# Four weight matrices loaded in 128-byte instead of 512-byte runs, with plain instead of spread columns, and GpSimd's combining of them moved ahead of four bias adds

## The reference

```python
def _sage_conv(x, src, dst, Wl, bl, Wr, num_nodes):
    msg = x[src]
    agg = jax.ops.segment_sum(msg, dst, num_segments=num_nodes)
    cnt = jax.ops.segment_sum(jnp.ones((src.shape[0],), x.dtype), dst, num_segments=num_nodes)
    agg = agg / jnp.maximum(cnt, 1.0)[:, None]
    return agg @ Wl.T + bl + x @ Wr.T
...
    h = jax.nn.relu(_sage_conv(x, src, dst, Wl1, bl1, Wr1, num_nodes))
    return _sage_conv(h, src, dst, Wl2, bl2, Wr2, num_nodes)
```

## Time and profile before

| | us |
|---|---|
| median of 3 runs | 357.29 (356.71 to 357.84) |
| the profiled execution's own time | 357.84 |
| its span, first to last instruction | 356.0 |
| PE busy | 343.8 (97%) |
| DVE busy | 248.0 (70%) |
| POOL busy | 137.6 (39%) |
| ACT busy | 85.4 (24%) |

### The profile page before, as it was taken

How to read it: one execution, slowest core, us unless ns; L and a number is a source line. 1 busy time by engine, 2 the same in 40 slices (tenths; PEclk the granted TensorE clock), 3 DMA queues, 4 the chain that set the end, 5 groups by cost and what they waited for, 6 DMA issues and landing times.

```text
span 356.0 us, 4336 instructions
## 1 busy us (share of the span) xinstructions
PE 343.8 (97%) x1617; PEld 243.5 (68%) x1617; DVE 248.0 (70%) x410; ACT 85.4 (24%) x185; POOL 137.6 (39%) x106
## 2 busy tenths in 40 slices
PE   8999999997999999999999999999958999999996
PEld 4459888783478888888888888645544544484454
DVE  5899999998798887940895507688875555454543
ACT  3556663414300000000011232303352332112110
POOL 5000000008599999999211110777034002622120
PEclk9999999999999999999999999999989999999999
DMA  7100004149400000150300499910000000000003
GB/s 239 55 3 2 3 2 165 74 156 327 168 0 2 0 1 2 22 215 2 88 0 2 151 218 197 218 43 0 0 1 2 0 1 0 2 0 0 2 0 120
DMA packets 18486, 22.07 MB, mean 62 GB/s; under 512 B 2016, under 2 KB 10720, under 8 KB 18464
## 3 DMA queue, kind: packets, MB, share of 16 engines
q1 hardware_dynamic: 17936, 20.85, 21.4%
q0 software_dynamic: 240, 0.79, 0.8%
q10 hardware_dynamic: 288, 0.13, 0.1%
HBM read 20.72 MB, written 1.05 MB: 61 GB/s over the span
## 4 chain that ended last, share of the span: by engine, by line
PE 69%; DVE 15%; SPq 7%; DMA 3%; issue 2%; ACT 2%; ACTq 0%; DVEq 0%
PE bank L1702 14%; PE bank L1592 14%; PE bank L1535 14%; SPq L847 7%; PE bank L604 4%; PE bank L1742 4%; PE bank L1478 4%; PE bank L577 4%; PE bank L1690 4%; PE bank L601 3%; DMA slots<-in_L_gnn_Wr 2%; DVE stats L1134 2%; DVE h L1186 2%; PE bank L593 2%; PE bank L1465 2%
## 5 line engine op out<-in xcount | busy, mean ns | idle before, releaser
L888 POOL TENSOR_TENSOR spare<-slots 128x512 f32<-128x512 f32 x4 | 6.0, 1491 | 76.1 <-PE bank L1478 75.4
L996 ACT ACTIVATE columns<-mean_var,eps 128x1 f32<-128x1 f32 x16 | 4.7, 294 | 123.9 <-DVE mean_var L1135 123.9
L1592 PE MATMUL bank<-slots,wall 128*128 128x256 f32 x128 | 30.2, 380 | 0.0
L1478 PE MATMUL bank<-h_t,spare 128*128 128x256 f32 x128 | 28.1, 379 | 0.0
L1658 PE MATMUL bank<-slots 128*128 128x512 f32 x64 | 28.0, 593 | 0.0
L604 PE MATMUL bank<-slots 128*128 128x112 bf16 x256 | 27.8, 229 | 0.0
L1358 DVE STREAM_TRANSPOSE wall<-slots 128x512 f32<-128x512 f32 x16 | 16.3, 1082 | 16.5 <-DMA slots<-in_L_gnn_Wl 13.8
L1592 PEld LDWEIGHTS bank<-slots,wall 128*128 128x128 f32 x128 | 24.2, 191 | 3.1
L1478 PEld LDWEIGHTS bank<-h_t,spare 128*128 128x128 f32 x128 | 24.2, 190 | 3.2
L601 PE MATMUL bank<-slots 128*128 128x140 bf16 x128 | 26.3, 242 | 0.0
L387 DVE TENSOR_TENSOR slots<-slots 128x1792 bf16<-128x1792 bf16 (+1 forms) x27 | 25.1, 987 | 0.0
(11 more groups left out here) (261 smaller groups left out, 765.2 us busy)
## 6 DMA issues: line engine op xcount, KB each, us to landing
slots<-in_L_gnn_W_rel SPq DMA_DIRECT2D x4, 1024.0 KB, 10.4
spare<-in_L_gnn_W_ffn SPq DMA_DIRECT2D x1, 2048.0 KB, 8.0
slots<-in_L_gnn_W_ffn SPq DMA_DIRECT2D x1, 2048.0 KB, 10.2
slots<-in_L_gnn_Wl SPq DMA_DIRECT2D x8, 256.0 KB, 9.9
slots<-in_L_gnn_Wr SPq DMA_DIRECT2D x8, 256.0 KB, 8.1
x<-in_x SPq DMA_DIRECT2D x4, 256.0 KB, 5.6
bias<-in_L_gnn_W SPq DMA_DIRECT2D x2, 512.0 KB, 5.3
slots<-in_L_gnn_W_self SPq DMA_DIRECT2D x1, 1024.0 KB, 5.3
```

The source lines that it names most:

```text
L1478: ins = pe.matmul(bank, left, right, start=start and i == 0, stop=stop and i == len(pairs) - 1)
L1592: ins = pe.matmul(into, left[:, k, tile(p)], right[:, k, :], start=(n in (0, 2, 3, 5) and r == 0 and k == 0), stop=False, skip_group_check ...
```

## The change

The feature index is now `t*128 + q*32 + k`: tile t holds 128 neighbouring columns. A source run is 32 columns, 128 bytes, and each quarter's DMA becomes four, one per tile. There are 64 DMAs of 64 KB instead of 16 of 256 KB. DVE's transposes read their source without a step, and so do PE's transposes of `h`. Independently of that, POOL's two `combine_own` come ahead of its four bias adds of the feed-forward output instead of behind them.

```diff
         def turned_rows(ap, quarter):
 
-            return ap.rearrange("(o i) (q c) -> q i o c", i=B, q=QB)[quarter]
+            return ap.rearrange("(o i) (t q k) -> q i t o k", i=B, q=QB, k=B)[quarter]
...
                 for quarter in range(QB):
-                    into = sage_raw[q][quarter * B:(quarter + 1) * B, :, :].rearrange("p a n -> p (a n)")
-                    sp.dma_start(into.rearrange("p (o c) -> p o c", c=D // QB), turned_rows(ap, quarter)).then_inc(sage_loaded[q], 16)
+                    into = sage_raw[q][quarter * B:(quarter + 1) * B, :, :].rearrange("p t (o k) -> p t o k", k=B)
+                    rows = turned_rows(ap, quarter)
+                    for t in range(KT):
+                        sp.dma_start(into[:, t], rows[:, t]).then_inc(sage_loaded[q], 16)
...
+            for layer in range(2):
+                combine_own(layer)
             for t in FFN_TILES:
                 pool.wait_ge(t_ready, use_of(H_FFN, t) + 1)
                 pool.tensor_tensor(h[:, t, :], h[:, t, :], bf2, ALU.add).then_inc(ffn_biased, 1)
             pool.wait_ge(late_rows_loaded, 16 * 3)
 
-            for layer in range(2):
-                combine_own(layer)
...
-                dve.wait_ge(sage_loaded[q], 16 * QB)
-                raw = sage_raw[q].rearrange("p a n -> p (a n)").rearrange("p (o c t) -> p t o c", t=KT, c=B)
-                dve.transpose(sage(q, k).rearrange("p (o c) -> p o c", c=B), raw[:, k]).then_inc(turned[q], 1)
+                dve.wait_ge(sage_loaded[q], 16 * QB * KT)
+                dve.transpose(sage(q, k), sage_raw[q][:, k, :]).then_inc(turned[q], 1)
...
-                spread = h[:, t, :].rearrange("p (c t) -> p t c", t=KT)
-                fill(use_of(what, t), [spread[:, k] if what in (H_SAGE1, H_SAGE2) else h[:, t, k * P:(k + 1) * P] for k in range(KT)])
+                fill(use_of(what, t), [h[:, t, k * P:(k + 1) * P] for k in range(KT)])
```

## The result

| | us |
|---|---|
| after, median of 4 runs | 375.03 (374.45 to 376.29) |
| before, median of 4 runs | 357.00 (356.60 to 357.84) |
| ratio, 95% interval | 1.0506 (1.0472 to 1.0541) |
| profiled execution of after, time and span | 376.56, 374.7 |

The change costs 18.0 us between the medians (16.9 to 19.3 by the interval of the ratio). The predicted 379.0 is 4 us too high, 375.03 lies within the range of 369 to 409, and the sign is as forecast.

What follows compares the result with a forecast made beforehand. The four weights' load was taken to set the start of DVE's feed-forward tiles and so the end. Load +13.3, POOL's wait +12.2 and relief -3.9 gave +21.6, predicting a 379 us median, range 369 to 409.

Steps and rivals of the forecast that it cites:

- What bounds it: The four weights' load sets DVE's first feed-forward tile; a microsecond later there is a microsecond at the end.
- POOL's wait, +12.2: After the last transpose, DVE's first feed-forward tile waits for POOL's four sums and two bias adds: +12.2 us.
- Contention relief, -3.9: DVE's first feed-forward tile falls from 11.08 to 7.17 us because POOL's sums are over by then: -3.9 us.
- The load, +13.3: Weight stream of 128-byte packets at 17 ns each takes 34.8 us instead of 21.5: +13.3 us.
- Packets or issues: In the weight load, packets bind at 34.8 us; SP's 64 issues of 0.48, 30.7 us, hide behind them.
- rival 1: Weight load: cheap packets, SP's issues bind, weights there by 236, +4.2; with POOL's +8.3 that is 370; chance 0.15.
- The forecast's own lower end: Weight packets at 13.4 ns need 27.4 us and are overtaken by SP's issues (30.7, +9.2): 375.3.
- Transposes, 0: Reading without a step gains DVE's four last transposes nothing; bound of 1.9 us gained, taken as 0.
- The clock: PE's longer stand before GCN may leave its clock low; nothing added, 1 us kept for it.
- Rival 3: Weight load: dear packets, over 20.4 up to 31.4 ns, stream up to 64.3 us, up to 409; chance 0.22.
- rivals 4 and 5: 4: stream speeds up to 384 GB/s, 353.4, chance 0.02; 5: sizes cancel or POOL's wait is hidden, chance 0.01.
- 428 us: Sum if every 128-byte weight packet were handled twice, at 2 x 20.4 = 40.8 ns; third rival's dear end.

Runs made afterwards that it cites:

- the two parts alone: Two kernels: after with POOL's order as before, 366.09 us (+8.5); before with only POOL's move, 365.76 us (+8.2).
- the move alone: The kernel before with only both groups of POOL's sums put ahead of the four bias adds; 365.76 us, ratio 1.0233.
- the new load and the old order: The changed kernel with its 64 short-run DMAs and step-free transposes, but POOL's bias adds ahead of the sums as before; 366.09 us, ratio 1.0234.
- 128 partitions: The kernel before with each weight DMA written to all 128 partitions instead of 32, 512-byte runs kept, last layer computing something else; 355.01 us, ratio 0.9930.
- two queues: The kernel before with the upper two quarters of each weight issued from ScalarE's queue, the lower two from SP; 354.81 us, ratio 0.9941.
- blocks of 32: The kernel before, 512-byte runs kept, with transposes reading blocks of 32 neighbouring elements and the feature order absorbed elsewhere; 356.24 us, ratio 0.9970.
- 16 short runs: The changed kernel's 128-byte runs and transposes, but 16 DMAs of 256 KB and POOL's order as before; 363.32 us, ratio 1.0175.
- 64 long runs: The kernel before with its 16 weight DMAs cut into 64 of 64 KB, runs still 512 bytes; 360.05 us, ratio 1.0068.

## Why the prediction was right, and where it was off

- **What bounds it: right.** Every microsecond at the first L1368 came through to the end: 14.55 us of wait and transposes, a later landing and a shorter tile explain the span to 0.2 us, and the two parts alone show the same at their medians (8.5 and 8.2).
- **POOL's wait, +12.2: right.** 12.05 us in after and 12.07 with the move alone. Recomputed from landing to L1368, 14.55 - 2.49 = 12.06.
- **Contention relief, -3.9: right**, 11.08 against 7.18, and 7.19 with the move alone. The relief follows the order of POOL and not the load: with the new load and the old order the tile takes 11.05.
- **The load, +13.3: too much, it measured +10.1.** The new stream was forecast well, but by luck. I took 17 ns, and 121 to 123 GB/s are 16 x 128 / 122 = 16.8 ns in after. That isn't the price of a packet, which is 15.2, but the pace of SP (below): a price 1.8 ns too high made up for an issue interval 0.05 us too short. What failed in the +13.3 is the step that set the new stream of 34.8 us against the old one of 21.5 and took the difference as the delay. From the opening of the queue (209.52, less the 2.1 of the start: 207.4) the new one took 34.5 to its landing (241.9), as forecast. The old one took 231.8 - 207.4 = 24.4 from the same point. Bytes over the rate of mid-stream leave out a stream's ends. Stretches of the kernel before show the rate leave 195 at the end, where the GCN weight (issued at 227.64) joins:

```profile
225.00:227.00 2.00, 2.00 (x11) 1.76 (x10) 0.78 (x1) 0.03 (x1) 1.92 (x2) 1.00 1.24 193
...
229.00:231.00 2.00, 2.00 (x6) 0.88 (x5) 1.35 (x2) 0.79 (x1) 2.00 (x2) 1.00 1.02 283
```

  The mixing is not the main reason, though. The trace also holds every packet with its size, and every report of a DMA engine that its part of a DMA has landed. In before the 512-byte packets that end per half microsecond fall from 184 to 129 at 228.0, and the first packet of the GCN weight moves at 228.72. The kernels with 128 partitions and with two queues have their four weights in before that weight is issued, and end as slowly: 281 packets in the half microsecond before 220.5 with 128 partitions, then 146, 66, 19, 19 and 9. The last counts are those of one engine alone (500 / 28.2 = 18). So the 16 DMA engines don't end together, and DVE waits for the last. Of the last 16 reports for the fourth weight the middle and the last lie 1.5 us apart in before (230.27, 231.79), 1.7 with 128 partitions (221.55, 223.20), 1.1 with two queues (223.27, 224.35) and 2.3 with blocks of 32 (229.96, 232.22), but 0.1 in after (243.93, 244.04) and 0.2 with 16 short runs (238.79, 238.97). By that estimate about half of the 2.9 us is this uneven end. Why the engines drift apart, and how the rest divides between the mixing and the start of the stream, isn't shown: no run took the GCN weight away. After the change it is issued at 242.38 and its first packet moves at 243.53, when the four weights are all but in.
- **Packets or issues: the right number for partly the wrong reason.** A packet costs 15.2 ns where the engines are full, 31.1 us for the stream, and after's 34 us are SP's. I had SP's floor at 64 x 0.48 = 30.7 and so hidden. The interval of 0.48 came from DMAs of 1 packet per partition. It is 0.475 with 128 packets per DMA and 0.53 with 512. By 0.48 the packets would have bound, narrowly (31.1 against 30.7). So the load is bound by issues, as rival 1 had it (chance 0.15), and not by packets of 17 ns. The forecast's own lower end, where the issues overtake the packets, was put at 375.3; that this is the result to 0.3 us is luck as well, since its stream of 30.7 for 34.5 and its old one of 21.5 for 24.4 largely cancel.
- **Transposes, 0: wrong, -1.6.** I had bounded them at -1.9 and took zero from the nearest row, PE's transposes (0.47 against 0.44), which say nothing about DVE. The row of a dense DVE operation of that size (0.55 against 1.02) was the nearer one. PE's own groups went from 0.47 to 0.44 as the rows said, and this fits the -0.2 of the last row of the account: from the end of the first tile to the end of the span it is 108.8 to 108.9 us in the kernels whose PE reads without a step (new load alone, 16 short runs, blocks of 32), and 109.1 in those that keep the step (the move alone, 64 long runs).
- **The sum of the steps.** 10.1 + 12.05 - 3.9 - 1.57 - 0.2 = 16.5. The two misses are 3.2 and 1.6 us in the same direction, and the medians give 1.5 back: 18.0. This last part isn't assigned. The intervals of the two single parts are 1.6 us either way, so it need not be anything.
- **The clock: no cost, as taken, but without margin.** After the longer stand PE is granted 0.50, the 1.2 GHz level, for the whole stretch from 264 to 286 us, and its mean is 0.968 instead of 0.995. PE's rows of after:

```profile
280.88 0.80 PE L1478 MATMUL bank<-adj,hi 128*128 128x512 f32 x1 [3.04 <-DVE h L1368]
...
287.58 1.10 PE L1478 MATMUL bank<-adj,hi 128*128 128x512 f32 x4
288.77 1.20 PE L1478 MATMUL bank<-adj,lo 128*128 128x512 f32 x4
```

  The backlog of GCN products ends at 287.58 + 1.10 = 288.68, and DVE's last split, which the next ones need, at 287.05 + 1.67 = 288.72. Before, PE had waited 0.89 us for it; the slow clock used all of that and no more.

**The rivals.** Rival 1 (issues bind, 370) had the mechanism of the landing right, and failed in two terms: the interval, 0.53 for 0.48 (62 x 0.05 = 3.1 us), and the opening of the queue at 204.0, since the issues stand twice more (1.16 and 2.30) until 207.4. Rival 3 fell: 15.2 ns isn't dear. So did rivals 4 and 5. The Trainium skill (DMA: Bandwidth & Descriptors, "Specifications") says that below 512 bytes the engines read, modify and write, for which the prediction had 428 us. The measured price is 15.2 ns, under the 20.4 that a single handling was allowed at most, so for source runs that end in one long piece per partition no such doubling shows.

**What is open.** SP stands for 1.84 us at 219.63 with nothing arriving for a microsecond (11 GB/s between 221 and 222); the kernel with 64 long runs has a like stand of 1.5 us near 218. I did not try what it is. Why the interval grows from 0.475 to 0.53 us with the packets of a DMA is open too.

## What to carry to other kernels

Before a layout is chosen to please its reader, count the packets and the issues of the load that feeds it, and ask whether that load's landing is on the path: 1.6 us saved on DVE's transposes cost 10.1 here, and the same 1.6 were to be had with blocks of 32 neighbours in long runs. Before work is moved ahead on an engine that looks idle, ask what its first instruction waits for: 2.5 us of bias adds, free where they stood, held all of DVE for 12 once they stood behind sums that wait for the last weight. And when a stream is replaced, time the old one from its start to its landing in the trace, with all that shares its queue, rather than by bytes over rate: its DMA engines need not end together, and DVE waits for the last.

## What the runs showed of the hardware

- One packet of a DMA engine cost 15.2 ns with 128 bytes, 42.0 with 512 (both to 32 partitions, one queue), 28.2 with 512 to 128 partitions. A quarter of the bytes saved 64% of the time: the short packet is far from as dear as the long one, and still 1.45 times as dear per byte.
- 32-partition DMAs on one queue ran at 195 GB/s; the same DMAs on two queues for different halves of the partitions at 272.
- Issues on SP, where the queue has room: 0.475 us apart with 128 packets per DMA, 0.53 with 512. Room in the queue goes by packets.
- The 16 DMA engines of a load don't end together: with 512-byte packets and a full queue the last report came 1.1 to 2.3 us behind the middle of the last 16, with 128-byte packets or a nearly empty queue 0.1 to 0.6.
- DVE's transpose of 128x512 f32 in blocks of 32: 1.07 us with a source step of 16 bytes, 0.67 without it, be the source contiguous (after) or in runs of 32 neighbours (0.67 for all 16 there too). The groups by line (min/median/max ns, first and last start) of before and of after:

```profile
L1358 DVE STREAM_TRANSPOSE wall<-slots x16: 1052/1071/1127, 214.7 to 234.8; 128x512 f32<-128x512 f32 x16
```

```profile
L1359 DVE STREAM_TRANSPOSE wall<-slots x16: 668/669/712, 217.3 to 245.9; 128x512 f32<-128x512 f32 x16
```

- POOL's sums of 128x1024 slow DVE's long operations with three operands to 2.0 to 2.7 us from 0.69 to 0.75, and hardly disturb its statistics (0.69 with and without).
- A lower granted clock costs only where PE is what the others wait for: 22 us at 0.50 cost nothing in after, 8 us at 0.74 to 0.83 some 1.2 us in the kernel with 128 partitions.
